# A scatter of edge rows with 128 rows in each indirect DMA instead of 125

## The reference

```python
edge_index = jnp.stack([src, dst])            # 50,000 edges, sorted by dst
h = jnp.maximum(_layernorm(x), 0.0)
x = x + L0(h, edge_index, edge_attr_16, ...)  # msg = relu(h[src] + edge_attr @ We + be); segment_sum by dst; a small MLP
h = jnp.maximum(_layernorm(x), 0.0)
x = x + L1(h, edge_weight, src, dst)          # 10 steps of h <- 0.9 * normalized A h + 0.1 * h0
h = jnp.maximum(_layernorm(x), 0.0)
x = x + L2(h, edge_index, edge_attr_3, ...)   # 3 layers: gated messages of (h[dst], h[src], edge_attr), segment_sum by dst
h = jnp.maximum(_layernorm(x), 0.0)
x = x + L3(h, edge_index, ...)                # silu of a linear map of (x_i, x_j - x_i), segment_sum by src
return x
```

## Time and profile before

| | us |
|---|---|
| median of three runs | 5595.54 |
| lowest and highest of them | 5579.65, 5604.30 |
| span of the profiled execution | 5635.3 |
| POOL busy in it | 3082.6 (55%) |
| of that the scatter at L755 (400) | 483.7 |
| of that the scatter at L728 (400) | 485.1 |
| of that the gathers at L770 (2080) | 2085.0 |
| PE busy | 3433.8 (61%) |
| DVE busy | 2812.2 (50%) |

### The profile page before, as it was taken

How to read it: one execution, slowest core, us unless ns; L and a number is a source line. 1 busy time by engine, 2 the same in 40 slices (tenths; PEclk the granted TensorE clock), 3 DMA queues, 4 the chain that set the end, 5 groups by cost and what they waited for, 6 DMA issues and landing times.

```text
span 5635.3 us, 80038 instructions
## 1 busy us (share of the span) xinstructions
PE 3433.8 (61%) x20001; PEld 2425.2 (43%) x20012; DVE 2812.2 (50%) x10008; ACT 928.0 (16%) x3266; POOL 3082.6 (55%) x3058
## 2 busy tenths in 40 slices
PE   2440078878889999656656556666566666344444
PEld 2330034444433444355556455555455556233333
DVE  7840088878621111355555455555555556533333
ACT  0000023333200000011112111112111112111111
POOL 3787676656688880145555345555255554355544
PEclk9999999989899999777777577777677777555555
DMA  4311123323599999411111211112111112011101
GB/s 139 82 26 9 47 67 74 83 70 80 133 331 344 356 352 356 165 40 43 42 43 42 38 41 43 42 43 41 38 43 43 42 43 40 18 20 19 19 18 21
DMA packets 293594, 498.20 MB, mean 88 GB/s; under 512 B 169174, under 2 KB 207203, under 8 KB 291962
## 3 DMA queue, kind: packets, MB, share of 16 engines
q1 hardware_dynamic: 118407, 339.94, 17.0%
q0 software_dynamic: 92160, 115.72, 11.2%
q10 hardware_dynamic: 82800, 40.01, 2.5%
HBM read 435.57 MB, written 58.97 MB: 88 GB/s over the span
## 4 chain that ended last, share of the span: by engine, by line
PE 38%; another core or an unknown queue 21%; DVE 14%; issue 13%; POOL 8%; ACT 2%; DMA 1%; DVEq 1%; ACTq 1%; SPq 0%; POOLq 0%
PE ps L1502 34%; POOL rows_dst L755 8%; DVE arena L1103 3%; DVE arena L1102 2%; PE ps L1728 2%; DVE arena L1121 1%; DVE arena L1119 1%; PE ps L1605 1%; DVE arena L1117 1%; DMA arena<-in_edge_attr_dram 1%; PE ps L1680 1%; DVE arena L1275 1%; ACT arena L1468 1%; DVE arena L1280 1%
## 5 line engine op out<-in xcount | busy, mean ns | idle before, releaser
L770 POOL DMA_INDIRECT arena<-table,arena x2080 | 2085.0, 1002 | 2200.4 <-DMA arena<-rows_dst 1299.9
L1502 PE MATMUL ps<-arena 128*128 128x96 f32 (+3 forms) x9176 | 1605.9, 354 | 573.3 <-issue 174.3
L1502 PEld LDWEIGHTS ps<-arena 128*128 128x128 f32 (+3 forms) x9176 | 1138.9, 207 | 953.3 <-issue 623.6
L1605 PE MATMUL ps<-ident,arena 128*96 128x128 f32 x416 | 149.9, 360 | 1123.1 <-ACT arena L1468 570.6
L1102 DVE TENSOR_SCALAR arena<-iota_row_b,arena 128x128 bf16<-128x128 bf16 x1664 | 438.3, 264 | 695.4 <-remote 518.6
L1502 PE MATMUL ps<-arena,nodes 125*64 125x500 f32 (+2 forms) x3144 | 649.6, 538 | 27.2 <-DVEq L1194 16.5
L755 POOL DMA_INDIRECT rows_dst<-stage,arena x400 | 483.7, 1209 | 196.3 <-issue 121.6
L1103 DVE TENSOR_SCALAR arena<-iota_row_b,arena 128x128 f32<-128x128 bf16 x2080 | 582.5, 298 | 0.0
L1605 PEld LDWEIGHTS ps<-ident,arena 128*96 128x96 f32 x416 | 65.3, 157 | 1190.5 <-ACT arena L1468 588.3
L1115 DVE TENSOR_TENSOR arena<-ps,arena 128x256 f32<-128x256 f32 x416 | 175.4, 422 | 787.3 <-remote 614.9
L728 POOL DMA_INDIRECT rows_src<-stage,stage_at x400 | 485.1, 1213 | 118.5 <-issue 116.6
(11 more groups left out here) (284 smaller groups left out, 3858.7 us busy)
## 6 DMA issues: line engine op xcount, KB each, us to landing
arena<-dense SPq DMA_DIRECT2D x240, 750.0 KB
nodes<-dense SPq DMA_DIRECT2D x60, 750.0 KB
dense<-arena ACTq DMA_DIRECT2D x150, 250.0 KB
arena<-table,arena POOLq DMA_INDIRECT x2080
arena<-dense SPq DMA_DIRECT2D x60, 500.0 KB
arena<-rows_dst SPq DMA_DIRECT2D x208, 96.0 KB
arena<-dense SPq DMA_DIRECT2D x6, 2000.0 KB
arena<-pair_rows SPq DMA_DIRECT2D x12, 976.6 KB
```

Source lines behind the costliest of these rows:

```text
L770: nc.gpsimd.indirect_dma_start(rows[:, u, k, 0:width], None, frm, bass.IndirectOffsetOnAxis(ap=p[:, c, j, c_other:c_other + 1].bitcast(I32 ...
L1502: return nc.tensor.matmul(to, lhsT, rhs, start=start, stop=stop, skip_group_check=True)
L1605: nc.tensor.transpose(to, pay[:, c, j:j + K, :].rearrange("p k c -> p (k c)"), ident[:]).then_inc(tr_ready, 1)
```

## The change

Each DMA of the first scatter now takes all 128 partitions of its column of `stage`, three more than there are edges in it. The three spare rows go to rows of their own behind the 128 x 416 that are read: the DRAM tensor is made longer by 3 x 400 rows (`rows_all`), and an iota at the start of POOL's program fills the whole table of positions (`pos_all`, 128 x 400), so that partitions 125 to 127 name those rows; the placing then writes partitions 0 to 124 over it as before. `stage` gets 128 partitions; the memsets of it (L694 to L696) cover them, and ACT's copies write the first 125 as before. The second scatter's copies and DMAs are written as `stage[0:EP]`, which is what they were.

```diff
-        rows_dst = nc.dram_tensor("rows_dst", [128 * T, C], F32).ap()
+        rows_all = nc.dram_tensor("rows_dst", [128 * T + (128 - EP) * EJ, C], F32).ap()
+        rows_dst = rows_all[0:128 * T]
...
-        stage = sb("stage", [EP, 2, SG, C])
+        stage = sb("stage", [128, 2, SG, C])
...
-        pos_dst = carve([EP, EJ], I32)
+        pos_all = carve([128, EJ], I32)
+        pos_dst = pos_all[0:EP]
...
+            nc.gpsimd.iota(pos_all, [[1, EJ]], base=128 * T - EP * EJ, channel_multiplier=EJ)
             nc.gpsimd.memset(earlier[:, :, 0:1], 0.0)
...
                         nc.gpsimd.indirect_dma_start(
                             to, bass.IndirectOffsetOnAxis(ap=stage_at[:, h, j:j + 1], axis=0),
-                            stage[:, h, j, 0:width], None).then_inc(scattered[h], 16)
+                            stage[0:EP, h, j, 0:width], None).then_inc(scattered[h], 16)
...
                         nc.gpsimd.indirect_dma_start(
-                            rows_dst, bass.IndirectOffsetOnAxis(ap=pos_dst[:, j0 + j:j0 + j + 1], axis=0),
+                            rows_all, bass.IndirectOffsetOnAxis(ap=pos_all[:, j0 + j:j0 + j + 1], axis=0),
                             stage[:, h, j, :], None).then_inc(scattered[h], 16)
...
-                nc.scalar.copy(stage[:, h, :, 0:DA], at16[:, js, :])
+                nc.scalar.copy(stage[0:EP, h, :, 0:DA], at16[:, js, :])
```

More of the change, by code:

```diff
@@ L718, in prepare @@
                         if hi_c is None and lo_c == other:
-                            nc.gpsimd.tensor_copy(stage[:, h, :, lo_c].bitcast(I32), part[:, js])
+                            nc.gpsimd.tensor_copy(stage[0:EP, h, :, lo_c].bitcast(I32), part[:, js])
                         elif hi_c is None:
-                            nc.gpsimd.tensor_copy(stage[:, h, :, lo_c], part[:, js])
+                            nc.gpsimd.tensor_copy(stage[0:EP, h, :, lo_c], part[:, js])
                         else:
-                            nc.gpsimd.tensor_copy(stage[:, h, :, lo_c:hi_c], part[:, js, 0:hi_c - lo_c])
+                            nc.gpsimd.tensor_copy(stage[0:EP, h, :, lo_c:hi_c], part[:, js, 0:hi_c - lo_c])
                     nc.gpsimd.tensor_copy(stage_at[:, h, :], places[:, js]).then_inc(staged, 1)
@@ L1356, in stage_rows @@
                     a.wait_ge(scattered[h], q // 2 * (16 * SG))
-                nc.scalar.copy(stage[:, h, :, 0:DA], at16[:, js, :])
[L1358 to L1361, removed]
+                nc.scalar.copy(stage[0:EP, h, :, 0:DA], at16[:, js, :])
+                nc.scalar.copy(stage[0:EP, h, :, C_ATT3:C_ATT3 + DB], at3[:, js, :])
+                nc.scalar.copy(stage[0:EP, h, :, C_W], wgt[:, js])
+                nc.scalar.copy(stage[0:EP, h, :, C_KEY], lo[:, 1, js])
+                nc.scalar.copy(stage[0:EP, h, :, C_OTHER].bitcast(I32), key_i[:, 0, js]).then_inc(staged, 1)
             a.wait_ge(at_loaded, 16 * 2)
```

## The result

The changed kernel takes 5687.5 us at the median of four runs (5687.2 to 5696.0); the kernel before took 5596.8 us on the same chip, also at the median of four (5579.7 to 5604.3). The ratio is 1.0181 (95% interval 1.015 to 1.0211): 91 us slower, where I had forecast 72.5 us faster and a range that ended at 5570.

A forecast was written before the change was run, and what follows sets the result against it. POOL's queue of 400 indirect scatters sets the pace up to about 700 us. Gains of 23.9 us before group 25 and 48.6 after make 72.5: 5595.5 - 72.5 = 5523 us, own range 5500 to 5547, wider range 5490 to 5570.

The forecast's parts named there:

- The price of a scatter: First scatter on POOL: 128 rows would cost 0.944 us instead of 1.187, saving 0.243 each.
- rival 1: First scatter: direction, not count, makes it dear; 128 rows cost 1.187 to 1.215 us, time 5596 to 5607; chance 0.11.
- Where the first half stops: Before group 25, POOL waits about 24 us for ACT's refill behind the root, resuming at 363.0; 23.9 us gained.
- The step that failed: Layer norm's variance on DVE, ahead of ACT's root: hangs on the second placing alone, stays at 356.5 us.
- Rival 3: At ACT's root: no stop, gain 96.7 us, time 5499; chance 0.03. Aside: slower placing loads could make the gain 63.
- The second half: Groups 25 to 49 of the first scatter: 200 scatters, each 0.243 us shorter, gain 48.6 us.
- whole at the end: From L1054 on, the program moves by whatever the scatter's end moves, so the stage's gain arrives whole.
- rival 4: First scatter's refills: landing outlasts a group's time, about 10.7 us for a 28 us slower kernel; chance 0.04.
- The other edits: Iota, memsets and spare rows cost next to nothing: iota about 0.46 us, spare rows 115 KB more written.

The follow-up runs named there:

- late128_q25: Against the kernel before: 125 rows per scatter in groups 0 to 24, 128 rows in groups 25 to 49; 5620.4 us (before 5646.2), ratio 0.9968.
- rows127: Changed kernel with 127 rows per scatter in place of 128, two spare rows; 6371.7 us (kernel before 5637.2).
- probe_late128: The probe, 160 written-out and 160 looped small memsets on DVE, added to late128_q25; written-out ones took 209 us, looped ones 103 us.

## Why the prediction was wrong

- **The price of a scatter: right.** 0.958 for the 0.944 that I took; the price goes by how the count divides, as I argued from the earlier trace rows, and rival 1 (the direction) falls. The gap stayed 0.30. L731, the second scatter, hardly moved, 1.178 for 1.187.
- **Where the first half stops: right in place, wrong in size.** ACT stands at the root, refills are queued behind it, POOL waits for the first of them. I put POOL's return at 363.0 us and its stop at 24 us; it came back at 506.9 after 133.5. So what comes before group 25, put at 23.9 us gained, lost 120.0 (506.9 against 386.9).
- **The step that failed** is the sentence that the variance "hangs on DVE's second placing", which "doesn't wait for the scatter at all, so it won't come earlier". It doesn't wait for it by any semaphore, and that holds in the changed kernel too. From that I took it to be untouched, and so I had 356.5 us as a fixed time. But DVE and PE can be slowed by what POOL does with no wait between them: the variance came 145 us later. Rival 3's aside named the direction (denser scatters could slow the placing's loads, a tenth of 96 us); the size was fifteen times that, and nothing points to the loads: the DMA share fell in both of the first stretches, the compares' stops are put down to issue, and a memset without any load was held up too.
- **A row that could have warned me** was among mine. I read the second placing's 96 us as DVE's own time. Its stretch has 51 us of DVE work and matmuls at 105 ns each, where the same matmuls cost 20.41 / 320 = 64 ns early in the scatter. Something held PE while POOL scattered, in the kernel before, and making POOL faster was bound to touch it.
- **The second half: right** in the stage (45 us in late128_q25, against 46 expected there; 48.6 in my sum for 200 scatters from group 25 on), but "whole at the end" failed: 18 us of them arrived, with an interval from 4 to 32. The layers behind L1054 are tied to the scatter by more than its end: in late128_q25 DVE was held up at the start of layer 0, where in the kernel before it was not.
- **The rivals.** The sign was rival 4's, to which I gave 0.04, the mechanism wasn't: it was to be a long landing of the scatters, and POOL's stops were for positions and for the root. What I left out is a rival by which a denser stream of indirect DMAs slows other engines' instructions.
- **The other edits.** The first piece of the placing comes 0.4 us later (61.5 us against 61.1), as put down for the iota (0.46); the spare rows show nowhere.

What stays open is the mechanism. One suspect was the queues of the kind "instruction". From 160 to 240 us the kernel before shows

```profile
q0 software_dynamic: 1697, 0.70, 8.8%
q8 instruction: 2, 0.03, 0.4%
q14 instruction: 4, 0.03, 0.1%
```

and the changed kernel

```profile
q0 software_dynamic: 1888, 0.73, 5.0%
```

and not one instruction packet, though over the whole run both kernels have the same number of them (82 on q8, 145 on q14). In the changed kernel the first q8 packets of the scatter come at about 150, 243 and 329 us, two in POOL's stops and one within a us of the third. That would fit instructions being kept out by back-to-back indirect DMAs, and it fits as well a DVE and a PE that need none since they hardly move. For DVE the probe speaks for the second: 103 memsets were held up in 145 us without any such packet. What does hold them up, why in steps of 0.70 us, why DVE and PE and not ACT, and why it outlasts POOL's work, no run here tells. Nor is the edge measured between 1.43 us (held up, spread over 16) and 1.49 (nearly free, spread over 5): there rate and spread still change together. rows127 stands apart: its scatters are 2.89 us apart, the compares have no stop on issue, and its first placing still ends 21 us later than before.

## What to carry to other kernels

An indirect scatter's price on POOL went here by the largest divisor of its row count up to 16, so padding a list to a multiple of 16 is worth trying; but the faster stream was a gain here only where DVE and PE had little to do, from group 25 on. Before making a queue faster, look at the engines beside it: if their instructions have idle time put down to "issue", or matmuls that cost twice what they cost elsewhere, they may already be paying for that queue, and an engine that waits for nothing is not for that reason untouched. And take a pace from a stretch without stops, never from the first and last start of a line.

## What the runs showed of the hardware

- Instructions of DVE that wait for nothing were started in steps of 0.70 us, or multiples, while POOL issued indirect scatters 1.25 to 1.39 us apart, and partly at 1.43; PE did 116 matmuls in 69 us where it had done 320. 160 memsets of 85 ns took 209 us beside scatters 1.26 us apart, and 25 us beside scatters 1.49 apart. At 1.69 and 1.91 us nothing of it is left at the compares.
- The steps outlasted POOL's work: in probe_late128 they went on for 11 us after its last gather, and in 145 us of them no instruction packet ran on any DMA queue.
- The price of one indirect scatter of up to 128 rows: 0.945 to 0.958 us where 16 divides the rows, 0.984 for 126, 0.990 for 100, 1.083 for 119, 1.187 for 125, 2.551 for 127.
- Gathers of 128 rows at the start of layer 0 either kept 1.25 us apart and held DVE up (38 instructions in 40 us), or were drawn out to 1.5 us and left it free (155); which of the two went by the scatters before them.
